# One tail block of a decoder kernel on Trainium2: the order of every engine's work shifted by one step, and activation tables chosen by hand

## The reference

```python
# L2 ffn: 2048 tokens, 4 heads, 8 picks each
sim = jnp.einsum('pbthn,hkpn->pbthk', q, keys)
sx, ix = jax.lax.top_k(sim[0], TOPK); sy, iy = jax.lax.top_k(sim[1], TOPK)
scores, pk = jax.lax.top_k(all_scores, TOPK)          # 8 of the 64 sums sx + sy
down, up = down_embed[indices], up_embed[indices]     # rows of a table of 4096 experts
w = silu(einsum('btd,bthkd->bthk', x, down)) * softmax(scores)
out = einsum('bthk,bthkd->btd', w, up) + silu(x @ Wg.T) * (x @ Wu.T) @ Wd.T
# L3 attn: u, v = split(x @ W_in); v = conv3(silu(v)); y = scan(a*h + b*v); out = (u * silu(y)) @ W_out; its own norm
# L3 xattn: 8 heads of 64 against a context of 120 rows, softmax, output projection
```

## Time and profile before

| | us |
|---|---|
| median of 3 runs | 3331.88 (3330.68 to 3333.36) |
| the profiled execution | 3331.43 |
| its span, first to last instruction | 3329.5 |
| first to last `gated` product of the 64 steps | 1919.7 to 3010.3 |
| the block's steps without picks | 3010.3 to about 3153.5 |
| mean granted TensorE clock, share of full speed | 0.856 |

### The profile page before, as it was taken

The page is one execution under the profiler, slowest core; times in us unless marked ns, Lnnn a source line. Parts: engine busy times, 40 slices in busy tenths (PEclk is TensorE's granted clock), DMA queues, the critical chain, the costliest instruction groups (busy, mean ns, idle before and its releaser), DMA issues. The chain is left out here.

```text
span 3329.5 us, 38556 instructions
## 1 busy us (share of the span) xinstructions
PE 2408.2 (72%) x14138; PEld 1613.7 (48%) x14145; DVE 1604.5 (48%) x4208; ACT 1152.2 (35%) x2006; POOL 785.7 (24%) x756
## 2 busy tenths in 40 slices
PE   6777699797776654768777656676777767677686
PEld 3534488544434324624444345555555555555432
DVE  3644200357437582456647643545444545432187
ACT  0233122200422321320245522455445455545343
POOL 1000200130010064510000065543444444530000
PEclk9888599899988777977998877888888888887798
DMA  7200255262043335543001251111111111100000
GB/s 171 63 18 0 105 184 180 75 144 83 23 86 110 127 123 186 161 146 57 11 17 63 90 113 38 38 40 28 34 31 37 34 31 40 33 22 13 13 0 25
DMA packets 127119, 232.26 MB, mean 70 GB/s; under 512 B 38809, under 2 KB 76569, under 8 KB 122592
## 3 DMA queue, kind: packets, MB, share of 16 engines
q1 hardware_dynamic: 73840, 125.12, 13.4%
q0 software_dynamic: 51952, 100.65, 10.1%
q10 hardware_dynamic: 1152, 4.19, 0.3%
HBM read 245.59 MB, written 66.72 MB: 94 GB/s over the span
## 5 line engine op out<-in xcount | busy, mean ns | idle before, releaser
L2827 POOL DMA_INDIRECT L2f_G<-in_L2f_table,L2f_idx x512 | 524.6, 1025 | 566.0 <-PE psum L2880 409.9
L2880 PE MATMUL psum<-L2f_G,L2f_diag 128*128 128x256 f32 x1024 | 340.8, 505 | 279.1 <-ACT L2f_diag L3077 279.1
L2880 PEld LDWEIGHTS psum<-L2f_G,L2f_diag 128*128 128x128 f32 x1024 | 262.3, 263 | 356.5 <-ACT L2f_diag L3077 293.8
L3257 DVE CUSTOM_DVE_ANT_0 L2f_junk<-L2f_G,L2f_X 128x256 bf16<-128x256 f32 x512 | 182.7, 421 | 1.7 <-DMA L2f_G<-in_L2f_table,L2f_idx 1.7
L3077 ACT ACTIVATE L2f_diag<-const,L2f_actd 128x128 f32<-128x128 f32 x528 | 161.2, 388 | 33.4 <-DVE L2f_actd L3270 33.4
L3263 DVE TENSOR_TENSOR L2f_h<-L2f_h,psum 128x256 f32<-128x256 f32 x64 | 26.9, 421 | 289.7 <-ACT L2f_h L3065 289.2
L1032 PE MATMUL psum<-constb 128*128 128x256 bf16 x512 | 81.9, 285 | 85.9 <-ACT L1a_PT L1199 24.8
L2251 POOL DMA_INDIRECT picks_x<-L1f_rows,L1f_put x64 | 70.8, 1107 | 242.1 <-ACT L1f_rows L2341 223.2
L2861 PE MATMUL psum<-xT,L2f_mw 128*128 128x256 f32 x512 | 123.3, 384 | 3.9 <-ACT L2f_X L3048 3.9
L1199 ACT ACTIVATE L1a_PT<-psum 128x1536 f32<-128x1536 f32 x32 | 46.4, 1451 | 207.1 <-PE psum L1167 207.1
L1512 PE MATMUL psum<-L0f_xeT,L0f_we 128*128 128x256 f32 x480 | 107.9, 384 | 0.9 <-DVE L0f_xeT L1547 0.9
(11 more groups left out here) (677 smaller groups left out, 5185.3 us busy)
## 6 DMA issues: line engine op xcount, KB each, us to landing
L1f_we<-in_L1f_w SPq DMA_DIRECT2D x32, 384.0 KB, 8.6
picks_x<-zeros SPq DMA_DIRECT2D x16, 544.0 KB, 9.1
L1f_xe<-picks_x SPq DMA_DIRECT2D x32, 272.0 KB, 2.8
picks_y<-zeros SPq DMA_DIRECT2D x16, 512.0 KB, 6.3
L2f_G<-in_L2f_table,L2f_idx POOLq DMA_INDIRECT x512, 2.8
slots_x<-zeros POOLq DMA_DIRECT2D x8, 512.0 KB, 7.6
L1f_wb<-in_L2x_w SPq DMA_DIRECT2D x1, 4096.0 KB, 12.1
L1f_g<-picks_y ACTq DMA_DIRECT2D x8, 512.0 KB, 12.7
```

The source lines that it names most:

```text
L2827: nc.gpsimd.indirect_dma_start(out=G[:, n % ROWS, :], out_offset=None, in_=ins["L2f_table"], in_offset=bass.IndirectOffsetOnAxis(ap=IDX[:, ...
L2880: mm = mm_(ps[:, MIX, 0:D], diag[:, i % 2, k, :], row[:, D:2 * D], start=(h == 0 and k == 0), stop=(h == HEADS - 1 and k == TOPK - 1))
L3257: e = VE.tensor_tensor_reduce(out=junk[:, k, :], in0=row[:, 0:D], in1=X[:, t % 4, :], scale=1.0, scalar=0.0, op0=ALU.mult, op1=ALU.add, ac ...
```

## The change

Only the three loops and the table loads differ. In the loop over steps, PE does `picks(i)` first and `cross(i, 1)` last; `cross(i, 0)` and `ssm(i)` lie between `queries` and `down(i)`. ACT does `gate(i)` in step i (it was at the end of step i - 1), then `weigh` and `diagonal` of step i + 1; `keep(t)` moves to the end of the tile's last step. DVE does `dot(i + 1)` ahead of `gated(i)`, then `weighted(i + 1)`. The first step's dots, weights and diagonals go ahead of the loops. `tables(own)` loads a set where the last one loaded by it was another: one set with log and exp, one with silu. The call stands behind the wait of the function that it serves.

```diff
@@ -3011,10 +3011,8 @@
                 pe.wait_ge(s["padded"].sem, s["padded"].at(3))
                 for i in range(END):
                     t, h = divmod(i, HEADS)
-                    cross(i, 0)
-                    if h == 0 and 0 < t <= NT:
-                        turn_back(t - 1)
                     if i < STEPS:
+                        picks(i)
                         if h == 1 and t + 2 < NT:
                             pe.wait_ge(s["pk_hid"].sem, s["pk_hid"].at(i + 1))
                             pe.wait_ge(s["pk_yadd"].sem, s["pk_yadd"].at(t))
@@ -3022,10 +3020,10 @@
                         if h == 2 and t + 3 < NT:
                             pe.wait_ge(s["pk_hid"].sem, s["pk_hid"].at(i + 1))
                             queries(t + 3)
+                    cross(i, 0)
                     ssm(i)
-                    if i < STEPS:
-                        picks(i)
-                    cross(i, 1)
+                    if h == 0 and 0 < t <= NT:
+                        turn_back(t - 1)
                     if i < STEPS:
                         pe.wait_ge(s["pk_hid"].sem, s["pk_hid"].at(i + 1))
                         down(i)
@@ -3035,10 +3033,19 @@
                             pe.wait_ge(s["pk_qe"].sem, s["pk_qe"].at(t + 4))
                         if i + 1 < STEPS:
                             up(i + 1)
+                    cross(i, 1)
 
             @block.scalar
             def _(act):
                 link = Chain(act, s["ln_ready"])
+                table = [""]
+
+                def tables(own):
+                    if own != table[0]:
+                        nc.scalar.preload_act_table_set(own)
+                        table[0] = own
+
+                LOGS, SILU = "natural_log_exp_and_others", "silu_and_others"
 
                 def evac_queries(t):
                     act.wait_ge(s["pk_q"].sem, s["pk_q"].at(t + 1))
@@ -3056,17 +3063,20 @@
 
                 def exps(t):
                     act.wait_ge(s["pk_cent"].sem, s["pk_cent"].at(t + 1))
+                    tables(LOGS)
                     nc.scalar.activation(sc[:, :, :], sc[:, :, :], ACT.Exp).then_inc(s["pk_prob"].sem, 1)
 
                 def gate(i):
                     act.wait_ge(s["pk_up"].sem, s["pk_up"].at(i + 1))
                     if i >= 2:
                         act.wait_ge(s["pk_part"].sem, s["pk_part"].at(i - 1))
+                    tables(SILU)
                     nc.scalar.activation(h_[:, i % 2, :], ps[:, UP, 0:CW], ACT.Silu).then_inc(s["pk_silu"].sem, 1)
 
                 def weigh(i):
                     act.wait_ge(s["pk_dots"].sem, s["pk_dots"].at(i + 1))
                     n = len(rows(i))
+                    tables(SILU)
                     nc.scalar.activation(act_d[:, i % 2, 0:n], dots[:, i % 2, 0:n], ACT.Silu).then_inc(s["pk_gate"].sem, 1)
 
                 def diagonal(i):
@@ -3161,27 +3176,28 @@
                     evac_similar(t)
                     exps(t)
                 evac_queries(2)
-                gate(0)
+                weigh(0)
+                diagonal(0)
                 act.wait_ge(s["padded"].sem, s["padded"].at(3))
                 for i in range(END):
                     t, h = divmod(i, HEADS)
-                    if h == 0 and 0 < t <= NT:
-                        keep(t - 1)
                     if i < STEPS:
-                        weigh(i)
-                        diagonal(i)
-                    cross(i, 0)
+                        gate(i)
+                    if i + 1 < STEPS:
+                        weigh(i + 1)
+                        diagonal(i + 1)
                     if i < STEPS:
                         if h == 1 and t + 2 < NT:
                             evac_similar(t + 2)
                         if h == 2 and t + 3 < NT:
                             evac_queries(t + 3)
+                        if h == HEADS - 1:
+                            keep(t)
+                    cross(i, 0)
                     ssm(i)
-                    cross(i, 1)
                     if i < STEPS and h == 3 and t + 2 < NT:
                         exps(t + 2)
-                    if i + 1 < STEPS:
-                        gate(i + 1)
+                    cross(i, 1)
                 s["ln_ready"].base += link.n
 
             @block.vector
@@ -3374,24 +3390,22 @@
                     best_keys(t)
                     best_pairs(t)
                     experts(t)
+                dot(0)
+                weighted(0)
                 for i in range(END):
                     t, h = divmod(i, HEADS)
+                    ssm_gate(i)
+                    if i + 1 < STEPS:
+                        dot(i + 1)
                     if i < STEPS:
                         gated(i)
-                    ssm_gate(i)
-                    if i < STEPS:
-                        dot(i)
-                    late = cross_at(i, 0)[1] == 10
-                    if not late:
-                        cross(i, 0)
-                    if i < STEPS:
-                        weighted(i)
-                    if late:
-                        cross(i, 0)
+                    if i + 1 < STEPS:
+                        weighted(i + 1)
                     if h == 0 and 0 < t <= NT:
                         add_mix(t - 1)
                         if t % 2 == 0:
                             add_dense(t // 2 - 1)
+                    cross(i, 0)
                     ssm(i)
                     if i < STEPS:
                         if h == 2 and t + 2 < NT:
```

## The result

The changed kernel took **3222.38 us** (median of 4 runs, 3220.58 to 3225.72) against 3332.62 (4 runs, 3330.68 to 3340.46) for the kernel before beside it: ratio 0.9666, 95% interval 0.9649 to 0.9684. The forecast was 3160, so 171 us were to go and 110 went. The profiled execution took 3225.72, 105.7 less than that of the kernel before; its span is 3223.9.

The account below looks back on a forecast made before the run. The prediction took a ring of waits between engines to bound the kernel. Savings of 86 (46 main steps), 30 (second part), 40 (opening) and 15 (tail), 171 in all off 3331.4, gave 3160 us, range 3090 to 3260.

Parts of the forecast that it names:

- opening: First 9 steps, without L3 work: bound by POOL's gathers once reordered, 102 us in place of 141.87, 40 saved.
- second part: The 8 steps with the scan alone, without cross: 30 us saved of 128.59.
- The ring: Main-part steps: PE, ACT, DVE and POOL each wait for the one before, 13.3 us a step at full clock.
- The ledger: Eight-step main period followed step by step: 122.1 us, 96 work and 26 waits; 128.4 with 6.3 for the clock.
- The clock: PE running at half clock after long waits: 6.3 us a main period, bounds nothing and 12.
- What is left is how late DVE enters a step: Main part: DVE's lateness after PE (L, 7.7 in step 1) delays pk_hid to L + 3.3 into the step.
- The rival of costly loads: Each remaining table load costs another 1.4 us behind its wait, six on the path a period: 3208 us; chance 0.04.
- the last sign: Would show it wrong: opening steps of 13 us or more, L2f_diag waits over 2 a step, or period over 138.
- Tables: ACT's table loads: 21 a period become 14, those behind waits paid; tail's 25 become 5, saving 15 us there.
- Convoy: In-order engines add waits, some 1.2 us a step more: period 138, total 3245 us; chance 0.15.
- Few waits: ACT hides the loads and PE's clock stays up: period near 118, total 3083 us; chance 0.11.
- slower: pk_hid behind a row of dots makes PE wait over 6 us a step: period 158 or more, 3361 at 163; chance 0.07.

Follow-up runs that it names:

- e5: Changed kernel with one gather a step in place of eight after the first 28 (sparse values not the reference's); 0.9318 of the kernel before, 3115.0 us.
- e4: Kernel before, order unchanged, with only the hand-placed table loads added; 0.9941 of the kernel before.
- e6: Changed kernel with DVE's product of h_ ahead of the next step's dots in place of behind them; 0.9676 of the kernel before.

## Why the prediction was right, and where its sum was off

Sign and range held, the forecast time was 62 too low. For each term: the forecast, the changed kernel, and e5, which is the same order with hardly any gathers (against the first trace of the kernel before).

| saved, us | forecast | changed | e5 |
|---|---|---|---|
| opening (to 2061.6) | 40 | 2.6 | 48.8 |
| second part | 30 | 15.7 | 35.0 |
| 40 steps, five periods (715.1 before) | 75 | 42.2 | 81.5 |
| last six steps (105.0 before) | 11 | 29.3 | 37.4 |
| tail (no gathers in it) | 15 | 17.1 | |

- **The ring** was the bound, as argued: the order alone gives 2.4%, and PE's wait for the diagonals is gone.
- **The ledger** came out for its period, and nearly for its steps, where signals are not held up, but with errors that cancel (next point). Rows of steps 1, 2, 6 and 7 of e5, and its sum:
```profile
2352.35:2379.33 26.98, 23.64 (x85) 16.65 (x85) 11.25 (x49) 6.41 (x14) 2.31 (x2) 0.73 0.03 7
2379.33:2389.74 10.41, 10.41 (x70) 9.23 (x68) 1.66 (x3) 7.14 (x17) 1.00 (x1) 1.00 0.04 10
...
2439.34:2451.61 12.27, 11.36 (x68) 9.12 (x67) 1.25 (x3) 10.53 (x20) 1.00 (x1) 1.00 0.03 8
2451.61:2467.18 15.57, 13.17 (x54) 10.92 (x53) 13.90 (x76) 7.13 (x18) 1.00 (x1) 0.89 0.01 3
...
sum 127.25, PE 107.85 PEld 84.56 DVE 66.63 ACT 64.92 POOL 8.44; mean PE 13.48 PEld 10.57 DVE 8.33 ACT 8.11 POOL 1.06
```
  Steps 6 and 7 are 12.3 and 15.6 (ledger 12.8 and 15.1), the period 127.3 for 128.4. In the changed kernel they are 17.0 and 19.1; there the table loads of z = 9 and z = 10 wait for late signals (remote, 5.3 and 3.3), and in e5 they don't.
- **The clock** was undersized and the waits oversized. The forecast's period was 96 of work, 6.3 for the clock and 26 of waits; e5 has PE busy for 107.9, so about 12 for the clock, the forecast's upper bound, and idle for 19.4. That 127.3 came so near 128.4 is luck. Step 1 shows it: PE works 23.64 there where the earlier trace rows has 16.89, mostly since behind the wait the key and value projections of cross run at 1.2 GHz (16 matmuls of the keys take 5.75, in the kernel before 3.25; the granted clock is 0.51 from 2359.77 to 2371.28 and 0.73 over the step). The wait itself is 3.4, not 7.3: in the changed kernel DVE's dots start 4.1 into the step, where the ledger had L = 7.7.
- **"What is left is how late DVE enters a step"** is the reading that e6 puts in doubt: taking the dots' 2.9 out of the way of `pk_hid` moved nothing in the whole. A chain over DVE and ACT fits this, but is not shown.
- **The opening: "The ring no longer holds POOL", and "The opening is then POOL's"** is the step that failed. POOL had its runs of 24, but it was not the bound: it was busy for 77.79 of 127.72 and still waited 22.3 for picks, 12.6 of them at once. PE and ACT stood for late signals: the two stalls of 12.8 and 19.5 are more than the 25.7 by which the nine steps passed 102, and with one gather a step the nine steps take 78.5. The 11.6 before the first product were overlooked. It is what the last sign listed, steps of 13 or more in the opening, was there for: they are 14.2.
- **The last six steps** have less or no `similar` and routing for further tiles; the ledger's period was carried over to them, which was 18 too little. That this is why they are shorter was not tried.
- **Tables.** A period has 14 loads and the tail 5, as counted:
```profile
L3045 ACT ACT_TABLE_LOAD x14 | 18.0, 1283 | 11.7 <-remote 8.6 <-PE psum L2861 1.5 <-PE psum L2892 1.3
```
```profile
L3045 ACT ACT_TABLE_LOAD x5 | 6.4, 1283 | 1.6 <-PE psum L2988 0.6 <-PE psum L2892 0.5 <-PE psum L2979 0.4
```
  The tail saved 17.1 for 15, and 14.9 with the tables alone (e4, 128.2). That loads behind waits are paid was right too: early ones gave 18.2 in the 46 steps, 22 expected. The rival of costly loads is wrong: in e5's trace the load of 2439.55 ends at 2440.83 and the exponential starts at 2440.85. The Trainium skill's drain of 1.38 us a switch (ScalarE: Activation LUTs, What ACT_TABLE_LOAD costs) is not seen in this case.
- **Rivals.** "Convoy" (period 138, 3245) came nearer to the size than the forecast but not by its mechanism: with the same in-order engines and hardly any gathers the period is 127.3, not 138. "Few waits" and "slower" did not come.

## What to carry to other kernels

An order that takes slack out of a kernel can make it feel delays that the slack had covered: look in the trace of before for what would be exposed, and test it by taking the suspect away in both kernels, since one of them alone can't tell a new cost from an old one. A sum that comes out right is no proof of its terms: compare work and waits one by one. Where gathers run on POOL beside a tightly coupled pipeline, a wait that gives them out in small portions may be worth more than letting POOL run ahead. A table load by hand belongs ahead of the wait of its activation, not behind it.

## What was not expected of the hardware

- While gathers run, signals between other engines can come late: with runs of 12 by 3.2 to 3.7 us, with runs of 24 by 12.7 and 19.5; with one gather a step no engine had such a wait in 700 us, in either kernel. A run of 44 in the first trace of the kernel before held up none. The run with the profile was the slowest of the four of the changed kernel, but by less than 6 us (3225.72, the lowest 3220.58), where the two stalls of the opening alone are 32: it is not the profile's doing. The Trainium skill says that a gather from this engine posts a signal from each of 16 DMA engines (DMA: Bandwidth & Descriptors, Why a DMA increments its semaphore by 16 and not by 1), and warns that a high rate of semaphore increments from one engine can deadlock another and that they should be spaced (VectorE: DVE Perf Modes, The TRN2 errata — SBUF-src ops pay a fixed extra latency per instruction). The second is near to what is seen, though here signals are only late. Whether these completion signals are the cause no run here shows.
- The same kernel had late signals in one trace and none in another (the earlier trace rows are of the latter). Whether the chip makes the difference is open.
